# Gathers issued earlier, expert sums ahead of the coattention maxima, and several small steps moved, in a two-layer gated kernel

## What is computed

```python
x = x + tanh(g_xattn[0]) * attention(layernorm(x), ctx)             # 16 heads, rope
x = x + tanh(g_ffn[0])   * mixture(layernorm(x))                    # 8 experts, top 2, and a shared MLP of width 256
x = x + tanh(g_xattn[1]) * coattention(layernorm(x), ctx)
x = x + tanh(g_ffn[1])   * bitffn(layernorm(x))                     # ternary weights, int8-like activations
# mixture: scores = sigmoid(logits); for each expert e: out += where(chosen, mlp_e(x) * wmean_e, 0); out += mlp_shared(x)
# coattention, per batch, with e the normalised rows and c the context:
Sim  = (e @ w1)[:, None] + (c @ w2)[None, :] + (e * w3) @ c.T + b
hq   = softmax(Sim, axis=1) @ c
hc   = softmax(max(Sim, axis=1)) @ e                                # one row for the whole batch
out  = concat([e, hq, e * hq, e * hc]) @ W_qv + b_qv
```

## Time and profile before

| | |
|---|---|
| median of 3 runs | 718.35 us (709.12 to 721.25) |
| the profiled execution | 717.9 us |
| its span, first to last instruction | 716.0 us |
| PE busy | 591.5 us, 83% |
| DVE busy | 462.9 us, 65% |
| POOL busy | 377.1 us, 53% |
| ACT busy | 343.6 us, 48% |
| mean granted PE clock | 0.902 of full speed |

### The profile page before, as it was taken

How to read it: one execution, slowest core, us unless ns; L and a number is a source line. 1 busy time by engine, 2 the same in 40 slices (tenths; PEclk the granted TensorE clock), 3 DMA queues, 4 the chain that set the end, 5 groups by cost and what they waited for, 6 DMA issues and landing times. The chain is left out here.

```text
span 716.0 us, 10198 instructions
## 1 busy us (share of the span) xinstructions
PE 591.5 (83%) x3238; PEld 376.5 (53%) x3238; DVE 462.9 (65%) x838; ACT 343.6 (48%) x618; POOL 377.1 (53%) x548
## 2 busy tenths in 40 slices
PE   4997899999999988978259987657779579986985
PEld 2663334444444347746159985426557365873553
DVE  4877788888888317576925531634667626579994
ACT  3554578888889854243226652322020211106564
POOL 9767658686643504827710006031625926278796
PEclk9997599999999969997569997969799889999999
DMA  8669946799945039102235636020100100000001
GB/s 276 172 226 272 194 50 89 162 261 271 275 158 210 1 116 390 39 26 97 97 105 184 191 116 207 9 89 0 57 2 23 37 0 1 1 0 9 30 34 48
DMA packets 46958, 81.03 MB, mean 113 GB/s; under 512 B 6364, under 2 KB 23520, under 8 KB 46144
## 3 DMA queue, kind: packets, MB, share of 16 engines
q1 hardware_dynamic: 35960, 60.12, 24.9%
q0 software_dynamic: 9120, 18.42, 14.0%
q10 hardware_dynamic: 1832, 1.90, 1.2%
HBM read 41.50 MB, written 38.80 MB: 112 GB/s over the span
## 5 line engine op out<-in xcount | busy, mean ns | idle before, releaser
L762 DVE TENSOR_REDUCE mx<-ps_f 128x2 f32<-128x1024 f32 x128 | 148.9, 1218 | 28.8 <-PE ps_f L678 27.6
L866 ACT ACTIVATE prob<-ps_s 128x512 f32<-128x512 f32 x256 | 135.6, 603 | 30.1 <-PE ps_s L696 17.1
L696 PE MATMUL ps_s<-q_stacks,k_stacks 53*128 53x512 f32 x256 | 91.2, 458 | 1.1 <-ACT prob L866 1.1
L1053 POOL DMA_INDIRECT back<-sorted_y,back_row x32 | 31.9, 997 | 81.6 <-DMA sorted_y<-own_y 72.2
L696 PEld LDWEIGHTS ps_s<-q_stacks,k_stacks 53*128 53x128 f32 x256 | 41.7, 192 | 60.8 <-ACT prob L866 39.1
L705 PE MATMUL ps_o<-prob,vst 128*32 128x512 f32 x512 | 71.5, 633 | 1.2 <-ACT prob L866 0.5
L678 PE MATMUL ps_f<-k_stacks,q_stacks 53*128 53x512 f32 x256 | 66.8, 484 | 6.8 <-DVE mx L762 4.6
L790 POOL TENSOR_TENSOR q_stacks<-minus,q_stacks 128x1024 fp32r<-128x1024 f32 x16 | 38.0, 2377 | 34.2 <-ACT minus L857 34.2
L1883 PE MATMUL ps_q<-ks,qs 128*128 128x256 f32 x128 | 35.2, 423 | 15.1 <-DVE hq L2020 14.3
L678 PEld LDWEIGHTS ps_f<-k_stacks,q_stacks 53*128 53x128 f32 x256 | 29.4, 199 | 32.6 <-DVE mx L762 28.9
L1209 POOL DMA_INDIRECT sorted_x<-qs,row_i x32 | 34.4, 1074 | 22.9 <-DVE row_i L1623 13.5
(11 more groups left out here) (349 smaller groups left out, 1482.1 us busy)
## 6 DMA issues: line engine op xcount, KB each, us to landing
sorted_x<-zeros SPq DMA_DIRECT2D x9, 2048.0 KB, 8.4
own_x<-sorted_x SPq DMA_DIRECT2D x40, 128.0 KB, 2.1
sorted_y<-own_y SPq DMA_DIRECT2D x40, 128.0 KB, 1.8
k_stacks<-room_k POOLq DMA_DIRECT2D x18, 256.0 KB, 6.1
q_stacks<-room_q POOLq DMA_DIRECT2D x18, 256.0 KB, 7.3
up<-in_up SPq DMA_DIRECT2D x10, 256.0 KB, 6.5
x<-in_x SPq DMA_DIRECT2D x4, 512.0 KB, 10.0
ctx_raw<-in_ctxTC SPq DMA_DIRECT2D x4, 512.0 KB, 7.1
```

The source lines that it names most:

```text
L696: pe.matmul(ps_s[n % 3][:, :], ks[rows(h), 2 * s + pair, kt * P:(kt + 1) * P], qs[rows(h), 2 * s + pair, :], start=True, stop=True).then_i ...
L762: dve.tensor_reduce(mx[:, f % 2, qt, 2 * pair:2 * pair + 2], ps_f[n % 2][:, :, :], AX_X, ALU.max).then_inc(used, 1)
L866: act.activation(prob[:, kt % 2, j, :], ps_s[n % 3][:, :], ACT.Exp, scale=SCALE)\
L1053: pool.indirect_dma_start(moe["back"][t][:, c, :], None, a["sorted_y"], bass.IndirectOffsetOnAxis(moe["row"][:, c, t:t + 1], 0))\
```

## The change

1. In phase_coattend DVE's `combine_rows(b + 1)` goes from behind the four maxima to a place ahead of the first one. POOL's statistics of batch b+1 go from behind `partition_all_reduce` to ahead of it.
2. Gathers: 16 in phase_experts where there were 12; at the start of phase_coattend the 8 of batch 2 where there were the 4 left of batch 1; in the first coattention batch the 8 of batch 3 where there were the 8 of batch 2; none in the second batch, where there were 8.
3. At the end of phase_experts ACT sums the four magnitudes behind all its work on chunks 2 and 3, and waits for the `w32` loads only there; before, it waited for them ahead of `silu(4)`. Its copy `keep_y(2)` goes behind `high_h(6)`.
4. At the start of phase_experts ACT runs a sigmoid on one column as its first instruction, so that the table load stands there; `high_d(E, NX)` goes behind `sigmoid(0)`. PE's `router(1)` goes ahead of `transposes(2)`.
5. POOL normalises only batches 0 and 1 in phase_project and makes the statistics of batch 2; DVE normalises batch 2 at the start of phase_experts.
6. Three constants leave the first loads and become two loads of their own at the start of phase_experts (`more`, `above`); DVE and PE wait for three small loads where DVE waited for one. The 35 semaphore clears go from SP's stream of phase_project to that of phase_experts, behind the small loads.

```diff
 phase_project, POOL
-            for b in range(B - 1):
+            for b in range(B - 2):
                 normalise_batch(pool, per, norm, b)
+            batch_statistics(pool, per, norm, B - 2)
 phase_experts, SP
             sp.dma_start(lb[:, :], a["lb"].to_broadcast([P, E])).then_inc(small_in, 16)
+            sp.dma_start(more[:, :], a["more"]).then_inc(small_in, 16)
+            sp.dma_start(above[:, :].bitcast(U16), a["above"]).then_inc(small_in, 16)
...
+            for old in used_up:
+                sp.sem_clear(old)
 phase_experts, POOL
-            gather_rows(pool, a, moe, range(0, QT + 2))
+            gather_rows(pool, a, moe, range(0, 2 * QT))
 phase_experts, PE
             router(0)
+            router(1)
             pe.wait_ge(norm["normed"], 3)
             transposes(2)
-            router(1)
 phase_experts, ACT
+            act.activation(warm[:, :], per["gates"][:, 0:1], ACT.Sigmoid)
             act.wait_ge(up_in, 16 * (NX + 1))
...
+            sigmoid(0)
             high_d(E, NX)
-            sigmoid(0)
...
-            act.wait_ge(w32_in, 16 * 2)
             for m in range(SH * FRONT, SH * B):
                 silu(m)
                 high_h(m)
-                i, half = divmod(m - SH * FRONT, 2)
-                wait(act, abs_done, m - SH * FRONT)
-                act.activation(wjunk[:, :], w32[i][:, half * INNER:(half + 1) * INNER], ACT.Abs,
-                               accum_out=wabs[:, half, i:i + 1]).then_inc(abs_done, 1)
-                if m % SH:
-                    keep_y(m // SH)
+                if m % SH == 0 and m // SH > FRONT:
+                    keep_y(m // SH - 1)
+            keep_y(B - 1)
+            act.wait_ge(w32_in, 16 * 2)
+            for i in range(2):
+                for half in range(2):
+                    wait(act, abs_done, 2 * i + half)
+                    act.activation(wjunk[:, :], w32[i][:, half * INNER:(half + 1) * INNER], ACT.Abs,
+                                   accum_out=wabs[:, half, i:i + 1]).then_inc(abs_done, 1)
 phase_experts, DVE
+            normalise_late(dve, per, norm, B - 2, norm["normed"])
             low_w(0)
...
-            dve.wait_ge(small_in, 16)
+            dve.wait_ge(small_in, 16 * 3)
 phase_coattend, DVE
                 own_part(b, v)
+                if not last:
+                    combine_rows(dve, per, moe, norm, b + 1)
                 maximum(b, 0)
                 updated(0)
                 for q in range(1, QT):
                     maximum(b, q)
-                if not last:
-                    combine_rows(dve, per, moe, norm, b + 1)
                 sim_maxima(b)
 phase_coattend, POOL
-            gather_rows(pool, a, moe, range(QT + 2, 2 * QT))
+            gather_rows(pool, a, moe, range(2 * QT, 3 * QT))
...
             for b in range(B):
+                if b + 1 < B:
+                    batch_statistics(pool, per, norm, b + 1)
                 pool.wait_ge(z_ready, b + 1)
                 pool.partition_all_reduce(z[:, 2, :], z[:, 1, :], P, bass.bass_isa.ReduceOp.max)\
                     .then_inc(zmax_ready, 1)
-                if b + 1 < B:
-                    batch_statistics(pool, per, norm, b + 1)
...
-                if b + 2 < B:
-                    gather_rows(pool, a, moe, range((b + 2) * QT, (b + 3) * QT))
+                if b == 0:
+                    gather_rows(pool, a, moe, range(3 * QT, T))
```

More of the change, by code:

```diff
@@ L1111, in phase_experts @@
         back_i, weights = moe["row"], moe["weights"]
+        more = sb("more", [P, C_MORE], F32)
+        above = sb("above", [P, P], BF16)
+        warm = sb("warm", [P, 1], F32)
         need = sb("need", [P, 6, E], F32)
@@ L1712, in _ @@
                     residual(m // SH - 1)
+                else:
+                    keep_y(m // SH - 1)
                 low_h(m)
@@ L2468, in build @@
                               up, up_low, w_high, down, down_low, d_high, w32, wabs, arrived["experts"],
-                              arrived["weights"], arrived["magnitudes"], gw, gw_in, small, room_clear, moe_rows)
+                              arrived["weights"], arrived["magnitudes"], gw, gw_in, small, room_clear, moe_rows, used_up)
         if stop > 2:
@@ L2553, in layout @@
     a["wg"], a["wu"], a["wd"] = (chunks(i[f"L1_ffn_w_{n}"].T).reshape(P, -1) for n in ("gate", "up", "down"))
-    a["c32"], a["c16"], a["trig"], a["qrows"], a["krows"] = constants()
+    a["c32"], a["c16"], a["more"], a["above"], a["trig"], a["qrows"], a["krows"] = constants()
     return a
```

38 lines of the change are left out of this document (20 added, 18 removed).

## The result

The changed kernel took 689.26 us (median of 4 runs, 686.89 to 691.03) against 718.13 us before: a ratio of 0.964, 95% interval 0.956 to 0.972. The forecast was 691.4 us. Its profiled execution took 690.73 us with a span of 688.8, 27.2 us less than before.

| stretch | before, us | after, us | difference | forecast |
|---|---|---|---|---|
| up to phase_experts | 299.3 | 297.1 | -2.2 | 0 |
| its start to the first scatter | 17.2 | 17.4 | +0.2 | +0.7 |
| first scatter to first block | 48.2 | 46.8 | -1.4 | 0 |
| first block to phase_coattend | 106.3 | 98.9 | -7.4 | -8.0 |
| coattention, batch 1 | 37.1 | 32.3 | -4.8 | -4.6 |

What follows compares the result with a forecast made beforehand. It took waits between PE, DVE and POOL in the first three coattention batches, and ACT's wait at the end of phase_experts, as the bound. -8.0 + 0.7 - 4.6 - 2.2 - 12.4 = -26.5, from 717.9 to 691.4 us; range 684 to 706.

Steps and rivals of the forecast that it cites:

- End of phase_experts, -8.0: Change 3: project(4) 5.0 us sooner, 2.2 from PE's clock, 0.8 from magnitudes leaving ACT's chain; 8.0 us saved.
- Start, +0.7: Start of phase_experts, changes 4 to 6: places of the first eight tiles, and so POOL's scatters, 0.7 us later.
- First batch, -4.6: First coattention batch: normalise no longer waits 4.5 us for POOL's statistics, next transposes come sooner; 4.6 us saved.
- Second batch, -2.2: Second coattention batch: POOL becomes the last wait, about 4.0 us at nz; 40.1 to 37.9 us.
- the clock as a rival of its own: PE idles at other places and keeps the lower clock level: 10.6 us more, 702.0 us; chance 0.10.
- Third batch, -12.4: Third coattention batch: loses gathers, waits at nz, for statistics and hq, and the low clock; 49.4 to 37.0 us.
- the forecast's pattern: Fourth batch as model of one without combine_rows, 33.5 us with the next transposes; with combine_rows ahead, 36.5 us.
- the 0.5 us for POOL's work beside combine_rows: Third coattention batch: 0.5 us added to the pattern for POOL's work beside combine_rows.
- a sign of being wrong (over 4 us): Coattention batches: the fourth maximum coming more than 4 us later in its batch would show the forecast wrong.
- Contention: Second and third batch: combine_rows and residuals slowed beside POOL's work, 7.2 us more, 698.6 us; chance 0.16.
- The wait only changes place: The coattention gives nothing; only the two ends of phase_experts count, 710.6 us; chance 0.13.
- slower: POOL's reduction sets every coattention batch, 6.0 us more in each of three, 728.6 us; chance 0.03.

Runs made afterwards that it cites:

- x1_tail_back: The changed kernel with change 3 undone, so ACT waits for w32 ahead of the silus again; 712.3 us, ratio to the kernel before 0.979.
- z1_tail_back: Again the changed kernel with change 3 undone, in another group of runs; 713.1 us, ratio to the kernel before 0.982.
- z3_warm_gone: The changed kernel without ACT's sigmoid on one column at the start of phase_experts; ratio to the kernel before 0.980.
- y0_after: The changed kernel itself, run again on another chip; 686.65 us, ratio to the kernel before 0.966.
- x4_gathers_alone: The kernel before the change with only the gathers moved sooner; ratio to the kernel before 0.9955.
- x2_combine_back: The changed kernel with DVE's combine_rows behind the four maxima again, POOL's statistics staying ahead of the reduction; ratio to the kernel before 0.997.
- z2_gathers_back: The changed kernel with the old places of the gathers; ratio to the kernel before 1.006.
- y1_interleave: The changed kernel with combine_rows cut in three, placed ahead of the first, second and third maximum; 686.03 us, ratio to the kernel before 0.966.
- y2_quant_split: The changed kernel with POOL's nine quantising instructions spread over gaps between products and places behind batches; 686.58 us, ratio to the kernel before 0.964.
- x3_stats_back: The changed kernel with POOL's statistics of the next batch behind the reduction again; four runs between 702.6 and 715.2 us, no ratio given.

## Why the prediction was right

**Result.** 691.4 forecast, 689.26 measured; the sum was -26.5 and came to -27.2. It is less exact than that looks: the priced stretches fell short by 3.1 and others gave 3.8, so the nearness of the total is in part luck.

**End of phase_experts, -8.0.** -7.4 over the whole stretch, with each step as written: silu(4) follows PE, 4.91 us of idle PE gone, the pairs at 0.63. Up to project(4) it gave 5.0 as forecast; the clock and the magnitudes, 3.0 together, gave 2.5. x1_tail_back and z1_tail_back bring the same wait and the same low clock back. The magnitudes and the four gathers cost nothing on this chip; on the slow chips the gathers' 0 was wrong by 4 to 6 us.

**Start, +0.7.** +0.2. The parts were mis-sized by tenths; z3_warm_gone measures the moved load at 0.7 and the rest of the change at -0.5. The first scatter came 17.4 us after the phase's start, not at the 17.9 named as a sign.

**First batch, -4.6.** -4.8 (-4.7 in y0_after). Its waits came as written, the first maximum 2.2 us later and no wait of normalise; the forecast names parts of 2.7 and 4.5 us but no sum that gives 4.6, so the figure itself can't be checked step by step.

**Second batch, -2.2.** The mechanism was right (POOL's chain becomes the last wait, nz waits 4.76 where 4.0 was said), the size came out as +0.1 in the first profile and as -1.7 to -2.2 in the four others with this coattention. What the first profile has besides is the clock: 1.7 us for two sets of products behind the wait. The forecast had the clock as a rival of its own, as if it were all or nothing; it is decided batch by batch. POOL's four parts ahead of the reduction add up to 25.0 us, not the 25.2 written.

**Third batch, -12.4.** -11.5 (-11.3 to -11.9 in the four others). The runs split it: 9.4 from the gathers alone, the rest from the pair of moves. Here the forecast's pattern was right to a few tenths, the 0.5 us for POOL's work beside combine_rows was too small. POOL is the last wait in this batch too: nz waits 0.81 us for it, behind a chain without idle time, whose normalisation took 9.0 us from its first statistics to the quantisation where it took 7.7 in the fourth batch, which has no combine_rows. The third similarity waits 3.46 us for the first exponential and the two behind it run at the low clock, 6.50 us. The fourth maximum then comes 5.9 us later in its batch than in the pattern, which the forecast had named as a sign of being wrong (over 4 us). It cost nothing: in z3_warm_gone the same two run at full clock, POOL's reduction comes at the same place (24.9 us into the batch in both), nz waits longer, and the batch takes 37.5 us against 37.9, in z1_tail_back 38.0.

```profile
561.56 4.03 PE L1878 MATMUL ps_SC<-ks 128*128 128x512 f32 x8 [3.46 <-ACT qs L2125]
577.26 0.16 DVE L2029 TENSOR_REDUCE nz<-z 128x1 f32<-128x4 f32 x1 [3.33 <-POOL z L2156]
```

A small misreading is in the pattern: the last hqT of the fourth batch ends at 630.4 by its row, not at 630.2.

**What was not forecast.** The first 2.2 us lie in phase_project. The granted clock and busy time of that stretch, before and after:

```profile
260.90:299.30 38.40, 33.69 (x192) 29.24 (x192) 23.10 (x64) 13.69 (x24) 19.03 (x53) 0.87 0.67 246
```
```profile
261.50:297.10 35.60, 30.18 (x192) 25.96 (x192) 22.82 (x64) 13.39 (x24) 15.30 (x45) 1.00 0.73 266
```

PE has the same 192 products and needs 3.5 us less, at the higher clock. The changed code of this phase took 35.6 us in five profiles and 36.5 to 38.4 in the seven others that have it, the old code 38.4 and 37.5. So the 2.8 is for the most part the chance of the clock; a small effect of change 5 is not excluded. The 1.4 us between scatter and first block, 46.7 to 47.0 in five profiles against 48.2 in the one of before, were not tested by themselves. x4_gathers_alone, which has the old code there, issues its 32 scatters in 41.1 us, the others on the slow chips in 41.6 to 42.3, so the old code is not slower as such; before took 43.8.

**Rivals.** Contention hardly showed on DVE: combine_rows took 3.37 and 3.51 us, z 1.96 in the second batch. It showed on POOL in the third batch, and strongly where combine_rows stands behind the maxima (8.54 us in x2_combine_back), so leaving that place is a part of the gain. The low clock took 1.7 us in the second batch of one profile, and 2.6 in the third that cost nothing; at the end of phase_experts it gave back about what was forecast. "The wait only changes place" is wrong for the pair of moves, and nearly right for combine_rows alone (2.0 us). The mechanism of "slower" showed in x2_combine_back (5.3 us over the gathers alone) and z2_gathers_back (135.0 us against 126.6 before): what stands in front of the reduction sets the batch as soon as its input is late.

## What to carry to other kernels

Two moves on two engines can each be worth little or less than nothing and be worth 8 us together; before dropping one that did not pay, run the four combinations. An instruction put ahead of a serial point must have its input there first: here the gathers were the condition, and without them the same order waited 9 us in each of two batches. When one of two chains into a point is shortened alone, nothing may be gained: with the maxima sooner PE stood idle and ran 2.6 us slower behind it (y1_interleave), and with POOL's chain shorter its work fell where it slowed DVE (y2_quant_split). And a slow stretch that ends before the last wait costs nothing: look first whether the batch got longer for it.

## What was not expected of the hardware

- The granted clock differs between executions of the same code: the same phase_project took 35.6 or up to 38.4 us, the same second batch 37.9 or 40.2. Differences of 3 us between two single profiles, in a stretch whose code is the same, say nothing.
- These chips differed around POOL's indirect DMAs: from the first scatter to the first block it took 47 us on some and 61 to 65 on others, though POOL issued them as quickly (1003 ns each in x2_combine_back, 1027 in the first profile). Behind the sixteen gathers ACT and DVE stood still there, DVE for 5.7 us in x3_stats_back, and the change, which adds gathers beside other work, gained 2% there (z3_warm_gone) instead of 3.6%.
- A DVE instruction beside POOL's quantisation can be stretched several times: combine_rows took 8.54 us in x2_combine_back instead of 3.37, the residual 1.91 instead of 0.48.
